# Folded normalisation, a rearranged preparation and a new order of TensorE's work in the node passes of a two-layer graph kernel

## The reference, cut to what matters

```
h1  = layernorm(x + embedding) * ln1_g + ln1_b
ff  = relu(h1 @ fc1_w + fc1_b) @ fc2_w + fc2_b
l0  = layernorm(h1 + ff) * ln2_g + ln2_b
x'  = layernorm(x + l0)
```

## Time and profile before

| | us |
|---|---|
| median of three runs | 2345.2 |
| lowest and highest run | 2344.7, 2351.29 |
| the profiled execution | 2347.2 |
| its span in the trace | 2345.3 |
| busy in the span: POOL | 1563.5 (67%) |
| DVE | 1442.4 (62%) |
| PE | 1405.4 (60%) |
| ACT | 743.2 (32%) |
| mean granted TensorE clock | 0.78 of full speed |

### The profile page before, as it was taken

The page is one execution under the profiler, slowest core; times in us unless marked ns, Lnnn a source line. Parts: engine busy times, 40 slices in busy tenths (PEclk is TensorE's granted clock), DMA queues, the critical chain, the costliest instruction groups (busy, mean ns, idle before and its releaser), DMA issues.

```text
span 2345.3 us, 31879 instructions
## 1 busy us (share of the span) xinstructions
PE 1405.4 (60%) x7344; PEld 1095.4 (47%) x7345; DVE 1442.4 (62%) x2992; ACT 743.2 (32%) x1511; POOL 1563.5 (67%) x1647
## 2 busy tenths in 40 slices
PE   5345655555655555555678566666666566566565
PEld 3134654554554555555566444444444344344443
DVE  2246977877877877878567444554554554544544
ACT  2143543444444344344366311111111111111111
POOL 4177777777777777775311177777777777777774
PEclk9657877778778777778799887777777877777777
DMA  4478555555555555554000122222222222222221
GB/s 167 133 180 280 172 156 172 156 156 172 155 155 173 155 155 173 155 156 151 10 33 36 45 60 63 65 64 63 65 64 63 65 64 65 63 64 65 62 64 45
DMA packets 148884, 255.37 MB, mean 109 GB/s; under 512 B 74541, under 2 KB 99809, under 8 KB 148717
## 3 DMA queue, kind: packets, MB, share of 16 engines
q0 software_dynamic: 65072, 160.39, 24.1%
q1 hardware_dynamic: 81906, 92.81, 12.9%
q10 hardware_dynamic: 1870, 1.78, 0.2%
HBM read 233.19 MB, written 28.04 MB: 111 GB/s over the span
## 4 chain that ended last, share of the span: by engine, by line
POOL 60%; issue 21%; DMA 6%; PE 6%; DVE 4%; ACT 2%; POOLq 1%; DVEq 0%; SPq 0%; ACTq 0%; PEldq 0%
POOL arena L706 31%; POOL arena L658 28%; DMA kvq_tab<-arena 3%; PE ps L1100 2%; PE ps L1119 1%; DMA arena<-kvq_tab,arena 1%; ACT arena L862 1%; DMA xs<-in_x_dram 1%; PE ps L1059 1%; DVE arena L1482 1%; PE ps L1130 0%; DMA arena<-d 0%; PE ps L988 0%; PE ps L1095 0%; DVE arena L1531 0%
## 5 line engine op out<-in xcount | busy, mean ns | idle before, releaser
L658 POOL DMA_INDIRECT arena<-kvq_tab,arena x784 | 748.3, 955 | 264.5 <-issue 263.3
L706 POOL DMA_INDIRECT arena<-y_tab,arena x784 | 739.8, 944 | 252.3 <-issue 238.3
L1059 PE MATMUL ps<-arena 128*128 128x136 f32 x1568 | 314.7, 386 | 416.5 <-DVE arena L1437 416.5
L1059 PEld LDWEIGHTS ps<-arena 128*128 128x128 f32 x1568 | 305.1, 290 | 431.4 <-issue 431.4
L928 ACT ACTIVATE arena<-arena 128x512 f32<-128x512 f32 x224 | 123.3, 572 | 795.4 <-DVE arena L1572 795.4
L1572 DVE TENSOR_TENSOR arena<-ps,arena 128x512 f32<-128x512 f32 x224 | 134.6, 620 | 352.4 <-DMA arena<-y_tab,arena 349.5
L1199 PEld LDWEIGHTS ps<-arena 128*128 128x128 f32 x1568 | 264.2, 243 | 163.6 <-ACT arena L928 97.7
L1199 PE MATMUL ps<-arena 128*128 128x128 f32 x1568 | 285.6, 336 | 30.3 <-ACT arena L928 29.7
L1186 PE MATMUL ps<-w1blk,eaT 113*128 x456 | 251.9, 640 | 0.6 <-ACT eaT L923 0.6
L1383 DVE TENSOR_TENSOR arena<-ps,arena 128x512 f32<-128x512 f32 x224 | 137.9, 616 | 170.4 <-DMA arena<-kvq_tab,arena 169.7
L1035 PE MATMUL ps<-arena 128*128 128x128 f32 x1596 | 209.3, 284 | 41.2 <-ACT arena L798 26.1
(11 more groups left out here) (242 smaller groups left out, 1997.5 us busy)
## 6 DMA issues: line engine op xcount, KB each, us to landing
arena<-d SPq DMA_DIRECT2D x58, 897.0 KB, 5.0
arena<-kvq_tab,arena POOLq DMA_INDIRECT x784, 2.8
arena<-y_tab,arena POOLq DMA_INDIRECT x784, 2.5
arena<-ea SPq DMA_DIRECT2D x60, 112.0 KB, 2.0
ea<-in_edge_attr_dram SPq DMA_DIRECT2D x2, 3125.0 KB, 18.9
y_tab<-arena SPq DMA_DIRECT2D x10, 625.0 KB
kvq_tab<-arena SPq DMA_DIRECT2D x6, 937.5 KB
arena<-kvq_tab SPq DMA_DIRECT2D x59, 64.0 KB, 4.3
```

What stands on the lines that cost most here:

```text
L658: g.indirect_dma_start(kv_s[:, r, t, :], None, kvq_tab.rearrange("n (a d) -> (n a) d", a=3), bass.IndirectOffsetOnAxis(ap=v3(idx, RING)[:, ...
L706: g.indirect_dma_start(yg_s[:, r, t, :], None, y_tab, bass.IndirectOffsetOnAxis(ap=v3(idx1, RING)[:, r, t:t + 1], axis=0)).then_inc(m_g[r] ...
L1059: last = mm(sums, hot_s[:, u, t, :], contrib_s[:, u, t * RW:(t + 1) * RW], start=(t == 0), stop=(t == G - 1))
```

## The change

- **Preparation.** The loads of x for groups 6 to 9 (k = 3 and 4) are issued by ACT, not SP. Store 9 is issued by ACT (`BY_ACT`). On POOL, store 2 comes behind the heads' way out and back and the small weight loads, stores 4 and 6 each later in the list, and the table's second step ahead of store 8. DVE makes chunk table 0 behind group 4's copies, not group 6's.
- **Folded normalisation.** ACT's first normalisation writes h1 without ln1_g and ln1_b. Once, ahead of the passes, DVE multiplies the rows of fc1_w by ln1_g, PE multiplies ln1_b by fc1_w, and ACT adds that to fc1_b as the relu's bias. POOL makes the residual, h1 * ln1_g + (ln1_b + fc2_b), in two operations, and adds ln2_b to x in a third. DVE's L1518, L1531 and L1535 are gone. Two small loads of ln1_g and ln1_b as columns are new.
- **Order on PE.** In a pass PE makes four of the five y tiles, then the transposes of mid's rows, which wait for ACT's normalisation (n_n1) and no longer for DVE (n_h1), then the last y tile.

The diff, with the unchanged lines left out but for the heads of functions and loops:

```diff
...
+        fc1b_all = sb("fc1b_all", [P, FC])
+        ln1_cols = sb("ln1_cols", [P, 2])
...
+        BY_ACT = (9,)
...
-        n_n1 = sem("n_n1")
-        n_h1 = sem("n_h1"); n_hTp = sem("n_hTp")
+        n_n1 = sem("n_n1"); n_xb = sem("n_xb")
+        n_b1 = sem("n_b1"); n_b1s = sem("n_b1s"); n_fc1 = sem("n_fc1"); n_hTp = sem("n_hTp")
...
-            for k in range(GROUPS // 2):
+            for k in range(3):
                 if k == 0:
...
             for i in range(GROUPS):
-                if i not in BY_POOL:
+                if i not in BY_POOL + BY_ACT:
...
                     for k, t in enumerate((ln1g, ln1b, fc2b, ln2g, ln2b)):
+                    for k, t in enumerate((ln1g, ln1b)):
+                        sp.dma_start(ln1_cols[:, k:k + 1], t.rearrange("(p a) -> p a", a=1)).then_inc(s_w4, 16)
                 if c == 2:
                     for k, w in enumerate((w1f, w1b)):
...
-            store_rows(2)
...
-            store_rows(4)
+            store_rows(2)
...
             for h, b in ((0, 0), (1, BASE1)):
-            store_rows(6)
+            store_rows(4)
-            pool.wait_ge(s_ea, 16 * 10)
-            pool.dma_start(firsts[1].rearrange("(b c) -> b c", c=1), marks(d1), allow_slow_non_contiguous=True).then_inc(s_first[1], 16)
+            pool.wait_ge(s_ea, 16 * 10)
+            pool.dma_start(firsts[1].rearrange("(b c) -> b c", c=1), marks(d1), allow_slow_non_contiguous=True).then_inc(s_first[1], 16)
+            store_rows(6)
+            pool.wait_ge(s_tabo[0], 32)
+            pool.dma_start(tab_sb[0][:, :], tabs[0].rearrange("(a e) f -> a (e f)", a=1)).then_inc(s_tabi[0], 16)
+            pool.dma_start(nj[0][:, :], negs[0].rearrange("(a e) -> a e", a=1).to_broadcast([P, TE])).then_inc(s_tabi[0], 16)
-            pool.wait_ge(s_tabo[0], 32)
-            pool.dma_start(tab_sb[0][:, :], tabs[0].rearrange("(a e) f -> a (e f)", a=1)).then_inc(s_tabi[0], 16)
-            pool.dma_start(nj[0][:, :], negs[0].rearrange("(a e) -> a e", a=1).to_broadcast([P, TE])).then_inc(s_tabi[0], 16)
             for k in range(KVR):
...
-            pool.wait_ge(s_w4, 16 * (12 + 2 * (EG - 1)))
+            pool.wait_ge(s_w4, 16 * (14 + 2 * (EG - 1)))
             def pool_pass(new, mid, old, out_):
                 if new is not None:
-                    pool.wait_ge(n_h1, new + 1)
-                    g.tensor_tensor(v3(h1c[:, ds((new % 2) * (GRP * D), GRP * D)], GRP), v3(h1, GRP),
-                                    rows[:, 2:3, :].to_broadcast([P, GRP, D]), ALU.add).then_inc(n_h1c, 1)
+                    x3 = v3(xs[:, ds(new * (GRP * D), GRP * D)], GRP)
+                    c3 = v3(h1c[:, ds((new % 2) * (GRP * D), GRP * D)], GRP)
+                    pool.wait_ge(n_v[0], new + 1)
+                    g.tensor_tensor(x3, x3, rows[:, 4:5, :].to_broadcast([P, GRP, D]), ALU.add).then_inc(n_xb, 1)
+                    pool.wait_ge(n_n1, new + 1)
+                    g.tensor_tensor(c3, v3(h1, GRP), rows[:, 0:1, :].to_broadcast([P, GRP, D]), ALU.mult).then_inc(n_h1c, 1)
+                    pool.wait_ge(n_h1c, scaled)
+                    pool.reg_add(scaled, scaled, 2)
+                    g.tensor_tensor(c3, c3, rows[:, 1:2, :].to_broadcast([P, GRP, D]), ALU.add).then_inc(n_h1c, 1)
                 if mid is None and old is None and out_ is None:
...
+            g.tensor_tensor(rows[:, 1:2, :], rows[:, 1:2, :], rows[:, 2:3, :], ALU.add).then_inc(m_pool, 1)
+            pool.wait_ge(m_pool, 1)
+            scaled = counter(pool, "scaled", 1)
...
+            x_rows = x.rearrange("(p t) d -> p t d", t=TILES)
+            span = 2 * GRP
+            for k in range(3, GROUPS // 2):
+                act.dma_start(v3(xs[:, :], TILES)[0:NT, k * span:(k + 1) * span, :], x_rows[:, k * span:(k + 1) * span, :]).then_inc(s_x[k], 16)
...
                     if j % 2 == 0:
+                if i in BY_ACT:
+                    act.wait_ge(s_ca, acts(i * GRP + GRP - 1))
+                    act.wait_ge(s_cv, vecs(i * GRP + GRP - 1))
+                    act.dma_start(by_row(kvq_tab, i * GRP, GRP)[:, :, 0:QKV], kvst_s[0:NT, slots[i][0], :, :]).then_inc(s_kvo[slots[i][0]], 16)
             def first_loads():
...
-            act.wait_ge(s_w4, 16 * (12 + 2 * (EG - 1)))
+            act.wait_ge(s_w4, 16 * (14 + 2 * (EG - 1)))
             def sqrt(k, at, norm):
...
             def relu(new, c):
-                             bias=fc1b_sb[:, c:c + 1]).then_inc(n_f1s, 1)
+                             bias=fc1b_all[:, c:c + 1]).then_inc(n_f1s, 1)
             def normalised(to, t3, norm):
                 for t in range(GRP):
...
                 if new is not None:
-                    normalised(v3(res, GRP), v3(res, GRP), norm1).then_inc(n_n1, 1)
+                    if mid is not None:
+                        act.wait_ge(n_hTp, mid + 1)
+                        act.wait_ge(n_h1c, mid * 2 + 2)
+                    normalised(v3(h1, GRP), v3(res, GRP), norm1).then_inc(n_n1, 1)
                 if old is not None:
+            act.wait_ge(n_b1, 1)
+            for c in range(FC):
+                a.activation(fc1b_all[:, c:c + 1], bank(4)[:, c:c + 1], ACT.Identity, bias=fc1b_sb[:, c:c + 1]).then_inc(n_b1s, 1)
+            act.wait_ge(n_b1s, FC)
...
-            pe.wait_ge(s_w4, 16 * (12 + 2 * (EG - 1)))
+            pe.wait_ge(s_w4, 16 * (14 + 2 * (EG - 1)))
...
             def pe_pass(new, mid, old, out_):
-                if mid is not None:
-                    pe.wait_ge(n_h1, mid + 1)
-                    if out_ is not None:
-                        pe.wait_ge(n_xT, out_ + 1)
-                    transposes(h1, n_hTp)
                 if old is not None:
                 if out_ is not None:
-                    for t in range(GRP):
-                        if t == GRP - 1 and mid is not None:
-                            pe.wait_ge(n_hT, mid + 1)
-                        last = mm(rows_y(t), nTx[:, t * P:(t + 1) * P], w1x[:, :])
-                    last.then_inc(n_y, 1)
+                    for t in range(GRP - 1):
+                        mm(rows_y(t), nTx[:, t * P:(t + 1) * P], w1x[:, :])
+                if mid is not None:
+                    pe.wait_ge(n_n1, mid + 1)
+                    transposes(h1, n_hTp)
+                if out_ is not None:
+                    if mid is not None:
+                        pe.wait_ge(n_hT, mid + 1)
+                    mm(rows_y(GRP - 1), nTx[:, (GRP - 1) * P:GRP * P], w1x[:, :]).then_inc(n_y, 1)
                 if mid is not None:
+                    if type(mid) is int and mid == 0:
+                        pe.wait_ge(n_fc1, 1)
+                        pe.wait_ge(n_b1s, FC)
                 if out_ is not None:
...
+            for c in range(FC):
+                last = mm(bank(4)[:, c:c + 1], fc1_sb[:, c * P:(c + 1) * P], ln1_cols[:, 1:2])
+            last.then_inc(n_b1, 1)
...
                     if j % 2:
-                if i == 6:
+                if i == 4:
...
-            dve.wait_ge(s_w4, 16 * (12 + 2 * (EG - 1)))
+            dve.wait_ge(s_w4, 16 * (14 + 2 * (EG - 1)))
             def statistics(t3, var, norm):
...
-            r3, q3, h3 = v3(res, GRP), v3(res2, GRP), v3(h1, GRP)
+            r3, q3 = v3(res, GRP), v3(res2, GRP)
             def dve_pass(new, mid, old, out_):
...
                 if old is not None:
-                    dve.wait_ge(n_h1c, old + 1)
+                    dve.wait_ge(n_h1c, old * 2 + 2)
...
-                    link(tt(q3, q3, rowb(4), ALU.add))
+                    dve.wait_ge(n_xb, old + 1)
...
                 if new is not None:
+                    if mid is not None:
+                        dve.wait_ge(n_n1, mid + 1)
-                    dve.wait_ge(n_n1, new + 1)
-                    link(tt(r3, r3, rowb(0), ALU.mult))
-                    if mid is not None:
-                        dve.wait_ge(n_hTp, mid + 1)
-                        dve.wait_ge(n_h1c, mid + 1)
-                    tt(h3, r3, rowb(1), ALU.add).then_inc(n_h1, 1)
+            dve.wait_ge(n_b1, 1)
+            ts(fc1_sb[:, :], fc1_sb[:, :], ln1_cols[:, 0:1], None, ALU.mult).then_inc(n_fc1, 1)
-            dve.wait_ge(m_pool, 2)
+            dve.wait_ge(m_pool, 3)
```

## The result

The change made the kernel slower: 2366.8 us, median of four runs (2364.9 to 2369.8), against 2345.2. The ratio to the runs of the kernel before is 1.0074, 95% interval 1.0062 to 1.0087 (the two medians alone would give 1.0092; by either the loss is clear). I had forecast 2324 and at most 2338. The profiled execution took 2369.8 us, span 2367.9: 22.6 us more than before.

The account below looks back on a forecast made before the run. The prediction took POOL's gathers to bound the edge loops, SP's queue rate the preparation, and the dependency chain the node passes. Preparation −18 and node passes −3.5 made −21.5: 2325.7 profiled, 2324 us as median, range 2312 to 2338.

Parts of the forecast that it names:

- The preparation, 18 us of gain forecast: Ahead of the first gather: relieving SP's queue brings that gather from 113.63 to 95.6 us, 18 us gained, between 10 and 26.
- Store against load is different: Preparation, 93 to 96 us: q1 wrote 0.40 MB while q10 read 0.39, so a store beside a load need not share.
- the price of moved bytes at q1's rate: Preparation: 2.24 MB taken off SP's queue save 27 us at 83 GB/s or 17 at 133, net 11 to 21.
- my second rival: Preparation: the queues share, so stores end only 0 to 8 us earlier; total 2334 to 2342, near 2338; chance 0.21.
- POOL's queue holds no store that ends last: Preparation: POOL's stores 2 and 4, some 10 and 5 us later, have cover and delay nothing.
- The hidden layer at T+4.65: Node pass, T being the end of ACT's normalisation: hidden layer starts at T+4.65 instead of T+5.07, 0.4 us gained a pass.
- which no y tile covers now: Node pass: ACT's copy of the transposes, 0.7 us, stands uncovered on the chain before the last y tile.
- From the hidden layer to the next T are 12.2 us: Node pass: the stretch from hidden layer to the end of ACT's next normalisation, 12.2 us in the kernel before.
- Nothing waits: Node pass: POOL's three 1.54 us operations and its 1.35 us copy, some 6 us of 17, delay nothing.
- rival 4: Node passes: PE's new idle of 0.75 us a pass lowers its clock, 47 us over eight passes, 2374 total; chance 0.05.
- PE's idle stretch shrinks to some 0.9: Between node passes: PE's idle falls from 2.07 us to some 0.9, an argument against the lower clock.
- Before the first pass: Ahead of the node passes: eight small matmuls (1.7 us), four ACT operations (0.3 each) and a handover cost +3 us.

Follow-up runs that it names:

- the two added stores: Kernel before, with group 7's store (0.96 MB) made a second time and waited for, on ACT's queue or on SP's: ratios 1.0026 and 1.0031.

## Why the prediction was wrong

**The preparation, 18 us of gain forecast, 2.7 us of loss measured.** The step that failed is "Store against load is different", and with it the price of moved bytes at q1's rate. I took the 0.39 MB that q10 read beside q1's store for proof that the queues have rates of their own. That held for this one load, of 128 partitions. The loads of x and the row stores, of 125 rows each, divide one rate of some 120 to 137 GB/s between SP's and ACT's queue, which q1 alone had reached already. This was my second rival, priced at 2338 with 0.21, and it was the right mechanism for this part. The Trainium skill (DMA: Bandwidth & Descriptors, "Issuing engines are not separate DMA queues") says that spreading DMAs over engines saves only issue time. For SP's and ACT's queue the equal 7 us of the two added stores agree with it. For POOL's queue beside SP's, 280 GB/s against 133 for SP's alone, the trace does not, and there the measurement decides.

Why even the bytes moved from the end to the idle start of ACT's queue gained nothing, the chain tells: "POOL's queue holds no store that ends last" was wrong too. The forecast put the heads at 46, behind POOL's small issues that end at 41.25. But the spread waits until the heads' way out has landed, and in the kernel before this was at 50.30. In the changed kernel it was at 53.78, since the loads of x on ACT's queue now ran beside it, and the heads were there at 61. Store 4 went out behind them at 58.20 instead of 41 and landed at 81.7. Group 8 waited for its slot, and group 9 behind it, so that store 9 was issued at 85.79, not 75. The table was late as well: nj was in SBUF at 90.0, not by 72 to 80. The index behind it took 23 us, not 11.7, with store 8 and store 9 both under way.

**The hidden layer at T+4.65**: right to 0.02 us. But it was measured against the wrong alternative. With DVE's two operations gone and the old order on PE it starts at T+3.57 (the run with the transposes first). The fold was worth 1.5 us on the chain, and the new order gave 1.1 of it back. The y tiles are on the chain in either order. With the transposes first they cover ACT's copy of the transposed rows; with the y tiles first nothing covers that copy, 0.7 us, nor the handovers around it. The forecast knew this price ("which no y tile covers now") and did not compare it with the order of before.

**"From the hidden layer to the next T are 12.2 us"**, taken as unchanged: 13.38. Of the 1.2 us that are missing 1.0 are L1533's, and the sentence that failed is POOL's "Nothing waits". I checked who waits for POOL's results and who stands behind it in its queue, and not which operations run beside it.

**The memsets**, which the prediction did not mention: POOL starts them later behind two more operations and then owes three instead of one. Pass 2 took 4.1 us more than before (21.4 instead of 17.3). That the memsets are the cause was shown by moving them: with POOL's add last and the transposes first, pass 2 fell from 21.4 to 16.1, the lower clock included.

**The clock, rival 4.** It came at a chance of 0.05, at 7 us instead of 47. "PE's idle stretch shrinks to some 0.9" was wrong: it was 1.95, against 2.07 before, and a second of 0.8 had come beside it. What the runs show: kernels whose pass was 17.45 or less at the full clock lost it in at most one of passes 3 to 8 (17.3 before, 17.45, 16.95, 16.46, 16.07). At 18.15 it was lost in five of six, at 18.05 in four of six in the changed kernel but in two of six in the run of the node part alone, with the same node passes. So a microsecond of waiting was often paid twice, once itself and once in clock, and how often varies from execution to execution. Whether the length of one idle stretch or their sum decides was not settled: the gap was 3.07 us at 18.15 and 1.95 at 18.05.

**Before the first pass**: +3 forecast. From the first gather to pass 0 it is 1.6 us more here and up to 6.8 more in other kernels with the fold, but 3.0 more in the run of the preparation alone, which has none; so its price is not settled.

**The range.** 2312 to 2338 was said not to take its bounds all at once. It does: 2345 − 26 − 8 is 2311, and 2345 − 10 + 3 is 2338.

## What to carry to other kernels

An engine that is idle is not free: before work moves to POOL, look at what DVE runs at that moment, and keep POOL's operations away from tensor_scalar operations and those with two SBUF inputs on the chain. Moving a DMA from SP's queue to ACT's bought an earlier start here, and no bandwidth; look at the share of the DMA engines that each queue keeps busy before you take a second queue for a second rate, and follow the small transfers that move back because of the move. When a fold removes work from a chain, try it first with the old order: the reordering that looks natural beside it (here the y tiles ahead) may spend the gain.

## What the runs showed of the hardware

**POOL against DVE.** Which pairs wait, from the timelines. Five of DVE's tensor_scalar on float32 in SBUF, 128x128 each: 1.38 us alone, 2.31 beside the end of one POOL operation and the copy, 3.56 beside two and the copy, 19.40 beside the memsets. Its scalar_tensor_tensor of two SBUF inputs, 128x5: 0.16 alone, 1.17 beside POOL's tensor_tensor, but 0.17 at 1158.71 us in the changed kernel, amid POOL's 10.73 us memset. An operation that was held ended 0.02 to 0.09 us behind POOL's. Its statistics (1.07 for five beside POOL's L688 at 1240.17, and 1.07 without) and the add with one input in PSUM (0.82) never changed. The Trainium skill (SBUF — State Buffer, "SBUF: two separate sides") has this as an exclusive lock on a port pair that GpSimd and VectorE share, taken by a DVE operation in a two-port mode, or by one with two SBUF inputs against a GpSimd operation that reads SBUF. Every pair above agrees, the memset, which reads nothing, among them.

**The clock.** In the kernel before with ln2_b's add on POOL, five of the six late passes fell from a granted 1.00 to 0.91 when a pass of 17.3 us grew by 0.85 us of waiting, with the same matmuls.

**DMA queues.** Loads and stores of 125 rows reached 133 GB/s on SP's queue alone, with 32% of the 16 DMA engines busy, and no more on SP's and ACT's queue together (120 and 121); with POOL's stores beside SP's it was 280, with 84% busy.
